# A two-layer graph network: layer 2 leaves each node's own loop out of its gathers, adds x1 at the quad's finish, and its bias moves to VectorE

## The reference

```python
src = jnp.concatenate([_s, _d, _loop]); dst = jnp.concatenate([_d, _s, _loop])
_o = jnp.argsort(dst, stable=True); src = src[_o]; dst = dst[_o]
# layer 1: relational sum with 16 relations over 8 bases
W = einsum('rb,bio->rio', w_comp, weight); h = einsum('ni,rio->rno', x, W)
x1 = layernorm(x + segment_sum(h[etypes, src], dst) + h_bias)
# layer 2: mean over the neighbours
agg = segment_sum(x1[src], dst); deg = max(segment_sum(1, dst), 1)
out = layernorm(x1 + x1 @ W_self + b_self + (agg / deg) @ W_neigh)
```

## Time and profile before

| | us |
|---|---|
| median of three plain executions | 4158.03 |
| the profiled execution | 4168.57 |
| its span, first to last instruction | 4166.8 |
| preparation, up to layer 1's first gather | 124.5 |
| layer 1 | 2453.7 |
| layer 2, first gather to the end of the last | 1502.3 |
| after the last gather | 86.3 |

### The profile page before, as it was taken

How to read it: one execution, slowest core, us unless ns; L and a number is a source line. 1 busy time by engine, 2 the same in 40 slices (tenths; PEclk the granted TensorE clock), 3 DMA queues, 4 the chain that set the end, 5 groups by cost and what they waited for, 6 DMA issues and landing times.

```text
span 4166.8 us, 43539 instructions
## 1 busy us (share of the span) xinstructions
PE 2500.4 (60%) x14995; PEld 2335.4 (56%) x14995; DVE 1477.6 (35%) x5002; ACT 376.6 (9%) x568; POOL 2558.8 (61%) x2702
## 2 busy tenths in 40 slices
PE   1557777766676767666677665145454545555547
PEld 0447666766676667666667665134444444444546
DVE  3323223222222232322232222145555554644423
ACT  1111111111111110101111111000000000000001
POOL 6565666666666666666666664666666666666661
PEclk6667777777777777777777777555555555555555
DMA  2923333333333333333333332111222222222221
GB/s 63 282 80 91 100 100 101 103 101 98 99 104 98 100 101 99 100 98 102 96 106 96 108 96 73 46 46 53 54 53 52 61 53 54 60 58 52 60 69 48
DMA packets 262580, 355.82 MB, mean 85 GB/s; under 512 B 48747, under 2 KB 192713, under 8 KB 262353
## 3 DMA queue, kind: packets, MB, share of 16 engines
q0 software_dynamic: 109584, 272.74, 23.7%
q1 hardware_dynamic: 152768, 80.24, 6.5%
HBM read 320.64 MB, written 44.99 MB: 88 GB/s over the span
## 4 chain that ended last, share of the span: by engine, by line
PE 41%; issue 31%; DVE 11%; another core or an unknown queue 11%; DVEq 1%; ACT 0%; SPq 0%; DMA 0%; ACTq 0%
PE zps L1546 12%; PE yps L1562 8%; PE yps L1555 6%; PE tps L1562 4%; PE tps L1555 3%; DVE acc L1376 3%; PE zps L1626 3%; DVE acc L1433 2%; PE tps L1537 2%; DVE acc L1298 1%; DVE acc L1356 1%; PE yps L1552 1%; PE tps L1644 1%; DVE acc L1437 1%
## 5 line engine op out<-in xcount | busy, mean ns | idle before, releaser
L1138 POOL DMA_INDIRECT rows<-x_x_rows,src_t x1469 | 1395.4, 950 | 843.6 <-issue 402.0
L1152 POOL DMA_INDIRECT rows<-x_rows,idx_l x837 | 793.6, 948 | 437.0 <-issue 237.2
L1546 PE MATMUL zps<-acc,rows 128*128 128x128 f32 x3328 | 600.5, 339 | 161.3 <-issue 156.7
L1546 PEld LDWEIGHTS zps<-acc,rows 128*128 128x128 f32 x3328 | 540.1, 247 | 179.2 <-issue 177.1
L1626 PE MATMUL zps<-acc,rows 128*128 128x64 f32 x1674 | 392.4, 413 | 161.5 <-issue 157.4
L1626 PEld LDWEIGHTS zps<-acc,rows 128*128 128x128 f32 x1674 | 374.8, 327 | 177.4 <-issue 176.3
L1562 PE MATMUL yps<-acc 128*128 128x128 f32 x2224 | 377.4, 318 | 149.4 <-issue 147.5
L1281 DVE TENSOR_TENSOR acc<-oh,tps 128x1024 f32<-128x1024 f32 x208 | 254.0, 1221 | 564.2 <-PE tps L1537 252.8
L1562 PEld LDWEIGHTS yps<-acc 128*128 128x128 f32 x2224 | 340.6, 230 | 178.6 <-issue 177.4
L1190 ACT COPY acc<-zps 128x1024 f32<-128x1024 f32 x208 | 210.5, 1012 | 2129.7 <-remote 1561.7
L1298 DVE TENSOR_TENSOR acc<-acc,yps 128x48 f32 (+1 forms) x1112 | 225.7, 203 | 493.9 <-remote 291.1
(11 more groups left out here) (199 smaller groups left out, 2115.4 us busy)
## 6 DMA issues: line engine op xcount, KB each, us to landing
rows<-x_x_rows,src_t POOLq DMA_INDIRECT x1469
rows<-x_rows,idx_l POOLq DMA_INDIRECT x837
acc<-in_edge_type_dram SPq DMA_DIRECT2D x207, 64.0 KB
x_x_rows<-in_x_dram SPq DMA_DIRECT2D x20, 576.0 KB
x_x_rows<-zrow SPq DMA_DIRECT2D x20, 576.0 KB
xin<-in_x_dram SPq DMA_DIRECT2D x24, 256.0 KB
x_x_rows<-xout SPq DMA_DIRECT2D x24, 256.0 KB
x_rows<-xout SPq DMA_DIRECT2D x24, 256.0 KB
```

Source lines behind the costliest of these rows:

```text
L1138: gather = pool.indirect_dma_start(out=wide_rows[:, g % WIDE_SLOTS, c, :], out_offset=None, in_=table, in_offset=bass.IndirectOffsetOnAxis ...
L1152: pool.indirect_dma_start(out=rows[:, j % SLOTS, c, :], out_offset=None, in_=x1_rows[0:n_nodes, :], in_offset=bass.IndirectOffsetOnAxis(ap ...
L1546: last = nc.tensor.matmul(zps[g % 2][:, c], slot_rows(g, c), a[:, g % 4, c], start=True, stop=True)
```

## The change

Layer 2 no longer gathers the loops. A loop is recognised as the last edge of its node: `flat` is the difference between the next edge's target and this one's, 1 at the last edge of a node and 0 elsewhere. Each edge so marked leaves the count of late edges, and the marks are turned and kept as `loops_b`. New tests (`orders`) ask that every difference is 0 or 1, that every marked edge has source = target, and that the first target is node 0; otherwise the plain program runs.

```diff
-FRONT = 20
+FRONT = 19
     def late_of(g):
-        return P * CPG * (1.0 - early_share * QUAD * front(g))
+        return P * CPG * (16.0 / 17.0 - early_share * QUAD * front(g))
...
+                nc.vector.tensor_tensor(flat[:, :, 0:P - 1], work1[:, :, 1:P], work1[:, :, 0:P - 1],
+                                        ALU.subtract).then_inc(s_order, 1)
...
+                nc.vector.tensor_reduce(loop_n[:, :], flat, AX, ALU.add).then_inc(s_order, 1)
...
+                nc.vector.tensor_tensor(lates[:, :], lates[:, :], loop_n[:, :], ALU.subtract).then_inc(s_order, 1)
...
+                for k, (q, m) in enumerate(quads):
+                    act.wait_ge(s_loops, k + 1)
+                    nc.scalar.copy(loops_b[:, q * P:(q + m) * P], tps[1][:, 0:m, :]).then_inc(s_loopc, 1)
```

```diff
+                    nc.vector.scalar_tensor_tensor(out=rel_t[:, 0:PLAIN * CPG], in0=loops_b[:, 0:PLAIN * CPG],
+                                                   scalar=float(4 * WIN), in1=rel_t[:, 0:PLAIN * CPG], op0=ALU.mult,
+                                                   op1=ALU.add).then_inc(ruled, 1)
...
-                        nc.vector.tensor_scalar(late_b[:, :], src_t[:, c0:c0 + unit_cols], float(full_rows), None,
-                                                ALU.is_ge).then_inc(step, 1)
+                        nc.vector.scalar_tensor_tensor(out=late_b[:, :], in0=src_t[:, c0:c0 + unit_cols],
+                                                       scalar=float(full_rows), in1=loops_b[:, c0:c0 + unit_cols],
+                                                       op0=ALU.is_ge, op1=ALU.subtract).then_inc(step, 1)
```

```diff
                     def quad_means(k):
...
+                        dve.wait_ge(n2.turned, k + 1)
+                        nc.vector.tensor_tensor(xin[:, k % 2, 0:m], xin[:, k % 2, 0:m],
+                                                bself_p.unsqueeze(1).to_broadcast([P, m, d]), ALU.add).then_inc(n2.rdeg, 1)
                         dve.wait_ge(w2.group_added, final_group(k) + 1)
+                        dve.wait_ge(n2.xt_ready, k + 1)
+                        own = mem[:, k * QUAD:k * QUAD + m * P]
+                        nc.vector.tensor_tensor(own, own, tps[1][:, 0:m, :].rearrange("p t e -> p (t e)"),
+                                                ALU.add).then_inc(n2.deg, 1)
+                        dve.wait_ge(n2.deg, k + 1)
                         nc.vector.tensor_tensor(stage[:, 0:m].rearrange("p t e -> p (t e)"),
...
-                            nc.tensor.matmul(tps[1][:, j, :], xt[:, j, :], ws[:, :], start=False, stop=False)
-                            last = nc.tensor.matmul(tps[1][:, j, :], onesm[0:1, :], bself[0:1, :], start=False, stop=True)
+                            last = nc.tensor.matmul(tps[1][:, j, :], xt[:, j, :], ws[:, :], start=False, stop=True)
```

More of the change, by code:

```diff
@@ L184, in gnn_kernel @@
         bias_col = sb("bias_col", [P, 1])
-        bself = sb("bself", [1, d])
+        bself = sb("bself", [P, d])
         wn = sb("wn", [P, d])
@@ L233, in gnn_kernel @@
         dst_i = halves[:, 0:chunks].rearrange("p (t e) -> p t e", t=etiles).bitcast(I32)
-        lo = stats[:, 0, :, :].rearrange("p a b -> p (a b)")[:, 0:etiles]
+        lo_and_end = stats[:, 0, :, :].rearrange("p a b -> p (a b)")[:, 0:etiles + 1]
+        lo = lo_and_end[:, 0:etiles]
+        flat = steps[:, :].rearrange("p (t e) -> p t e", t=etiles)
+        apart = halves[:, 0:chunks].rearrange("p (t e) -> p t e", t=etiles)
+        scratch = sums[:, 0:chunks]
+        next_chunk, next_tile = xt[:, 2, :], xt[:, 3, :]
         hi = stats[:, 1, :, :].rearrange("p a b -> p (a b)")[:, 0:etiles]
@@ L325, in gnn_kernel @@
         s_chk = sem("s_chk")
+        s_next = sem("s_next")
+        s_order = sem("s_order")
+        s_loops = sem("s_loops")
+        s_loopc = sem("s_loopc")
         table_in = sem("table_in")
@@ L396, in _ @@
                 act.wait_ge(s_set, len(quads))
+                act.wait_ge(s_loopc, len(quads))
             @block.vector
@@ L423, in _ @@
                 nc.vector.tensor_scalar(tri_b[:, :], lanes[:, :], part_f[:, 0:1], None, ALU.is_gt)
+                nc.vector.tensor_scalar(next_chunk, lanes[:, :], 1.0, part_f[:, 0:1], ALU.add, ALU.is_equal)
+                nc.vector.tensor_scalar(next_tile, lanes[:, :], 1.0 - P, part_f[:, 0:1], ALU.add, ALU.is_equal)
                 nc.vector.tensor_scalar(tri64[:, :], lanes[:, :], part_f[:, 0:1], None, ALU.is_ge).then_inc(s_dl, 1)
@@ L468, in _ @@
                 dve.wait_ge(s_dl, 24)
-                nc.vector.scalar_tensor_tensor(out=lates[:, :], in0=padding[:, :], scalar=28.0, in1=lates[:, :],
+                nc.vector.scalar_tensor_tensor(out=lates[:, :], in0=padding[:, :], scalar=20.0, in1=lates[:, :],
                                                op0=ALU.mult, op1=ALU.add).then_inc(s_dl, 1)
@@ L481, in _ @@
                 dve.wait_ge(s_dl, 29)
[L482 to L483 removed]
+                nc.vector.tensor_reduce(orders[:, 0:1], steps[:, :], AX, ALU.max).then_inc(s_dl, 1)
+                nc.vector.tensor_reduce(orders[:, 1:2], due[:, :], AX, ALU.max).then_inc(s_dl, 1)
                 nc.vector.tensor_reduce(verdict[:, 3:4], expected[:, :], AX, ALU.max).then_inc(s_dl, 1)
                 nc.vector.tensor_reduce(wide, padding[:, :], AX, ALU.max).then_inc(s_lo, 1)
+                nc.vector.tensor_tensor(apart, apart, flat, ALU.mult).then_inc(s_order, 1)
+                nc.vector.tensor_reduce(orders[:, 3:4], steps[:, :], AX, ALU.min).then_inc(s_order, 1)
+                dve.wait_ge(s_order, 6)
+                nc.vector.tensor_reduce(orders[:, 4:5], apart.rearrange("p t e -> p (t e)"), AX, ALU.max).then_inc(s_order, 1)
                 dve.wait_ge(s_dl, 32)
[L487 removed]
+                nc.vector.tensor_scalar(orders[:, 0:1], orders[:, 0:1], -1.0, None, ALU.add).then_inc(s_order, 1)
+                nc.vector.tensor_scalar(orders[:, 3:4], orders[:, 3:4], -1.0, None, ALU.mult).then_inc(s_order, 1)
+                nc.vector.tensor_scalar(orders[:, 2:3], verdict[:, 3:4], -float(SHIFT - WIN - 2 * QUAD), None,
                                         ALU.add).then_inc(s_dl, 1)
                 dve.wait_ge(s_dl, 33)
[L490 removed]
+                dve.wait_ge(s_order, 9)
+                nc.vector.tensor_reduce(late[:, 0:1], orders[:, :], AX, ALU.max).then_inc(s_dl, 1)
+                dve.wait_ge(s_dl, 34)
+                nc.vector.tensor_tensor(late[0:1, 0:1], late[0:1, 0:1], lo[0:1, 0:1], ALU.max).then_inc(s_order, 1)
                 for k, (q, m) in enumerate(quads):
@@ L582, in _ @@
                         last.then_inc(s_tr, 1)
+                    if k == 0:
+                        nc.tensor.matmul(next_lo, next_chunk, lo, start=True, stop=False)
+                        nc.tensor.matmul(next_lo, next_tile, lo_and_end[:, 1:etiles + 1], start=False,
+                                         stop=True).then_inc(s_next, 1)
                 pe.wait_ge(s_tot, 1)
@@ L604, in _ @@
                         last.then_inc(s_tr, 1)
+                pe.wait_ge(s_order, 2)
+                pe.wait_ge(s_relc, len(quads))
+                for k, (q, m) in enumerate(quads):
+                    if k:
+                        pe.wait_ge(s_loopc, k)
+                    for j in range(m):
+                        last = nc.tensor.transpose(tps[1][:, j, :], flat[:, q + j, :], ident[:, :])
+                    last.then_inc(s_loops, 1)
         nc.all_engine_barrier()
```

44 lines of the change are left out of this document (26 added, 18 removed).

## The result

The kernel after takes 4053.17 us (median of 4 runs, 4041.53 to 4059.01), the kernel before, run beside it, 4160.38 us (4 runs, 4150.41 to 4167.5): a ratio of 0.974, with an interval of 0.972 to 0.976. The forecast was 4090. The profiled execution took 4041.53 us, its span is 4039.7 us against 4166.8: 127.1 us less. The two profiles come from opposite ends of their kernels' executions (the fastest of four after, one slower than any of the plain ones before), so they lie 127 us apart where the medians lie 107.

What follows compares the result with a forecast made beforehand. GpSimd's layer-2 gathers set the pace, against always full slots. From the profiled 4168.57 us, -111 + 50 - 11 + 5.5 = -66.5 gave 4102; against the plain median 4091.5, stated as 4090 us, own range 4050 to 4130.

Steps and rivals of the forecast that it cites:

- The wait, +50: Quad's finish on VectorE: waiting for turned x1 and ScalarE's copy costs 2.5 us at each of 20 quads, +50 us.
- idle time of 8 to 15 us per quad: Sign of a right forecast: VectorE idles this long ahead of the bias or own-sum add.
- rival A: VectorE's new wait is free, since full slots stop GpSimd and the consumer catches up: 4041 us, chance 0.20.
- Fewer columns, -111: Layer 2's gathering on GpSimd: 953 columns for 1029, 76 gathers less at 1.460 us each, -111 us.
- Rival C: Layer 2's gathering stretch follows the consumer and its sorting, not the columns: 4165 us, chance 0.07.
- Denser sorting: The same 184 `pick` turns over 97 instead of 106 groups: costed at nothing, hidden in VectorE's idling; uncovered +20 us.
- The last gather was to be 55 to 65 us earlier: Sign of a right forecast: layer 2's last gather comes this much earlier.
- The bias: 196 bias passes leave TensorE: nothing while gathers run, -15.8 us after the last gather; together with the own-sum add -11.
- 4.4: After the last gather, the last three quads' own-sum add and `stage` stand behind the copy: +4.4 us.
- -11: Work behind layer 2's last gather: -15.8 us for bias passes and +4.4 for the last three quads, together -11 us.
- The preparation, +5.5: Ahead of layer 1: ScalarE's four copies behind its fill, with TensorE's turns, cost +5.5 us, between +2 and +16.

Runs made afterwards that it cites:

- b_wait: Kernel before, plus VectorE waiting for ScalarE's `xt` copy ahead of each quad's `stage`: ratio 0.9997 to before, 4159.03 us.
- a_out3: Kernel after with `xout` one group earlier, so VectorE waits a second time per quad: ratio 0.9758 to before, against 0.9742 of the kernel after.
- a_early: Kernel after with TensorE turning each quad's x1 as soon as its bank is free, to take VectorE's wait away: ratio 0.9744 to before.
- a_cols: Kernel after with `FRONT` 16 instead of 19, so 999 layer-2 gathers instead of 953: ratio 0.9888 to before, 61 us slower than after.
- b_again: Kernel before run once more unchanged, for a second profile: 4148.68 us in one run, gathering stretch 1498.38 us.
- a_bias_pe: Kernel after with layer 2's bias back on TensorE and no bias add on VectorE: ratio 0.9813 to before, 30 us slower than after.
- a_slots6: Kernel after with 6 instead of 8 slots for layer 2's gathered groups: ratio 0.9700 to before, 4029.9 us, 17 us faster than after.

## Why the prediction was right, and where it was not

The forecast named 4090 us, with 4050 to 4130 as its own case's range; 4053.17 lies 3 us inside its lower edge. The direction and most of the working held; one step, the wait, failed. That the range took the result in although 50 us of its middle were wrong is luck as much as width.

**The wait, +50: failed.** The step "a VectorE wait of this length costs 2.5 us, so 20 quads cost 50" is refuted by b_wait, a_out3 and a_early. Two things were wrong. The 2.5 us came from the worst place of the trace: the excess of the earlier trace rows exists at six pauses, 1.2 to 2.9 us each above the usual 3.5, not at each of 20 quads, and where it is gone (b_wait) others have come and the sum of the pauses is the same. And the wait was counted as added, though the same reading showed VectorE standing later for the products of this very copy: once `stage` waits for the copy, the products have all they need, and the wait ahead of `xout` falls from 257.5 to 20.6 us. What was right is that it would show as idle time of 8 to 15 us per quad: 203.4 us in 19 stretches, 10.7 each. This is rival A, the new wait is free, held at 0.20; its time, 4041, is 12 us from the median. The reason that A gave for it isn't shown.

**Fewer columns, -111: right.** 953 gathers, 1.449 us each. The price per column holds by a_cols (1.35 to the profile). The rest, 121.2 - 111 = 10, is in part the spread between profiles (b_again 4 us); what the other 6 are isn't shown. Rival C is out. Denser sorting cost nothing.

The last gather was to be 55 to 65 us earlier, which was -111 + 50; with the wait gone it is 120.6 us.

**The bias: 0 while gathers run, right; behind them -16, mis-sized.** a_bias_pe puts it at -27.1. The term took 0.72 us a tile for the pair of passes and 5.5 quads; a tile takes 1.02 less, the bias add costs nothing, 7 quads are left, and the last gather finds the consumer 10 us less behind. Against it the tail grew by 106.90 - 86.30 = 20.6 us, where the forecast had 4.4. The reason is read from the timelines: with narrower units the last quads are finished 2 groups apart, so 7 instead of 6 are left behind the last gather, one more at 15.1 us, and each of the three uncovered ones takes 1.1 to 1.6 us more for the own sum (14.3 us apart for 12.7). Together 19 to 20. The sum, -6.5 for -11, is right only because two errors met.

**The preparation, +5.5: right,** +5.1 between the two profiles. Layer 1's 65th gather starts at 120.5 to 124.5 us in the three profiles with the old preparation and at 129.4 to 131.3 in the seven with the new one up to a_slots6, so 8 is the better figure, inside the +2 to +16.

In sum -121.2 - 6.5 + 0.6 = -127.1 us in the profile, against -66.5 forecast; 50 of the 60.6 us between them are the wait. The 0.6 owes much to the chance of two profiles: with the 15.3 us of the means in its place the sum is -112.4, near the -107.2 between the medians.

**What stays open.** On the chips of the result the consumer takes 11.6 us a group whatever it does in them: not its passes (a_bias_pe), not VectorE's waits, not the slots. Nor is it its work as such, since behind the last gather it does a group in 6.5 to 7.1 us. On another it does one in 10.9 us or less and the pauses vanish from unchanged code. Whether that is the chip or something in that session was not found; of the smaller step, from 4155 to 4101 us, both sides were taken on the same chip (number 9), 12 minutes apart, so the chip alone doesn't make it. What holds back a signal from the fifth gather after a pause on is open too, and the kernel after itself was not run on the fast one, so what the change brings there is unmeasured. If gathers go there at 1.25 us, its 76 columns are an estimated 95 us of 3470.

## What to carry to other kernels

A wait that is moved ahead of another of the same cause doesn't add: follow what the later wait was for before pricing the new one, compare the engine's idle time of the whole stretch and not of one line, and never multiply the worst instance of a stall by the count of places. Where a producer runs ahead by a fixed number of slots, extra work of the consumer doesn't show while the producer runs; it shows behind the last transfer, so price it there, per group of debt, and try fewer slots. A pace that no edit of the program moves may lie outside the program: run the kernel before beside each experiment.

## What the hardware did that I had not expected

The same kernel, before, took 4155 to 4160 us beside most experiments, 4101 beside two and 3470 on another chip. There GpSimd started its gathers 1.27 us apart in layer 1 and elsewhere 1.53, with the same 0.95 us busy each.

In the kernel after, a turned x1 that was ready when at most 4 gathers had started since GpSimd's pause was mostly copied within 0.2 us, and one that was ready at 5 to 11 waited 10 us or more.

More slots made it slower and fewer made it faster, 7 us per group of lead, with an unchanged pace of 1.449 us per gather.
